# Reordered fill, drain and end of a two-layer graph-attention and expert kernel, with a merged routing softmax and moved attention products at the round borders

## What is computed

```python
x = x + gnn0(_layernorm(x), adj)   # masked attention over leaky_relu(f_i + f_j), softmax, @ Wh, elu
x = x + ffn0(_layernorm(x))        # per-token router (softmax, top 2 of 6), 6 experts of 3 layers, weighted
x = x + gnn1(_layernorm(x), adj)   # as gnn0 with other weights
x = x + ffn1(_layernorm(x))        # per-graph router on the mean token (top 2 of 8), gelu experts 128-256-128,
                                   # then a layer norm with gamma, beta
```

## Time and profile before

| | |
|---|---|
| median of 3 runs (lowest, highest) | 628.02 us (622.9, 629.22) |
| the profiled execution, its own time | 626.22 us |
| its span, first to last instruction | 624.2 us |
| PE busy / DVE / ACT / POOL | 563.5 (90%) / 459.6 (74%) / 411.5 (66%) / 233.8 (37%) us |
| steady body (mean of 12 between 95 and 405.2 us) | 25.85 us, PE busy 25.16, DVE 22.09, ACT 19.58 |
| tail, 16 groups | 7.14 us each, PE busy throughout |

### The profile page before, as it was taken

How to read it: one execution, slowest core, us unless ns; L and a number is a source line. 1 busy time by engine, 2 the same in 40 slices (tenths; PEclk the granted TensorE clock), 3 DMA queues, 4 the chain that set the end, 5 groups by cost and what they waited for, 6 DMA issues and landing times.

```text
span 624.2 us, 15150 instructions
## 1 busy us (share of the span) xinstructions
PE 563.5 (90%) x3830; PEld 455.1 (73%) x3831; DVE 459.6 (74%) x1714; ACT 411.5 (66%) x1099; POOL 233.8 (37%) x450
## 2 busy tenths in 40 slices
PE   5778999999999999999999999988966799999992
PEld 4555777777777777777777777766644599999992
DVE  2586778888898898988888888776453347777675
ACT  1244667767878678777777777857722178888782
POOL 5222213342434423344233442231332015666665
PEclk9988999999999999999999999999997799999997
DMA  8414225052250531404314043022000377777732
GB/s 189 95 37 153 66 89 154 2 153 72 83 152 1 151 98 54 152 15 137 101 51 152 10 142 102 1 104 102 1 1 1 93 244 217 231 220 223 216 112 67
DMA packets 78935, 66.19 MB, mean 106 GB/s; under 512 B 10018, under 2 KB 64562, under 8 KB 78898
## 3 DMA queue, kind: packets, MB, share of 16 engines
q1 hardware_dynamic: 65312, 59.78, 31.9%
q10 hardware_dynamic: 13586, 5.98, 3.6%
HBM read 61.31 MB, written 4.42 MB: 105 GB/s over the span
## 4 chain that ended last, share of the span: by engine, by line
PE 29%; DVE 17%; DMA 14%; issue 14%; ACT 13%; POOL 5%; SPq 5%; ACTq 1%; DVEq 1%; POOLq 0%
DMA x<-in_x 11%; PE bank L1547 4%; PE bank L1537 4%; SPq L612 4%; PE wide L1537 4%; PE wide L1547 4%; ACT p_xn L120 3%; PE bank L1340 3%; DMA w_scratch<-wrow 2%; PE bank L1353 2%; ACT h L785 2%; DVE h2w L1005 2%; DVE at_prT L317 2%; DVE route_stats L88 2%; ACT at_lk L284 2%
## 5 line engine op out<-in xcount | busy, mean ns | idle before, releaser
L1340 PE MATMUL bank<-h,w 128*128 128x512 f32 x192 | 101.4, 610 | 4.8 <-ACT h L790 4.8
L1353 PE MATMUL bank<-w,h2w 128*128 128x128 f32 x768 | 103.1, 278 | 0.0
L1353 PEld LDWEIGHTS bank<-w,h2w 128*128 128x128 f32 x768 | 95.0, 192 | 3.1 <-issue 1.0
L785 ACT ACTIVATE h<-bank,b 128x512 f32<-128x512 f32 x96 | 66.3, 690 | 43.8 <-PE bank L1340 43.8
L790 ACT ACTIVATE h<-bank,b 128x512 f32<-128x512 f32 x96 | 65.9, 687 | 27.6 <-PE bank L1334 27.6
L1005 DVE TENSOR_TENSOR h2w<-h,wide_w 128x512 f32<-128x512 f32 x96 | 65.1, 678 | 12.8 <-ACT h L785 12.6
L1332 PE MATMUL bank<-xnTh,w1h 128*128 128x512 f32 x96 | 67.3, 701 | 0.0
L101 POOL TENSOR_TENSOR route_var_eps<-route_mean_var,eps 128x4 f32<-128x4 f32 x16 | 10.9, 681 | 123.5 <-DVE route_mean_var L94 123.5
L101 POOL TENSOR_TENSOR at_var_eps<-at_mean_var,eps 128x4 f32<-128x4 f32 x32 | 12.3, 384 | 98.2 <-DVE at_mean_var L94 98.2
L269 ACT ACTIVATE at_pr<-at_lk,at_nm 128x128 f32<-128x128 f32 x128 | 41.1, 404 | 6.9 <-DVE at_nm L304 6.9
L240 PEld LDWEIGHTS wide<-at_wh,at_prT 128*128 128x128 f32 x256 | 31.9, 196 | 14.4 <-issue 5.2
(11 more groups left out here) (233 smaller groups left out, 1407.6 us busy)
## 6 DMA issues: line engine op xcount, KB each, us to landing
wide_w<-w_scratch SPq DMA_DIRECT2D x96, 256.0 KB, 4.5
mask<-in_L_ffn_W SPq DMA_DIRECT2D x128, 128.0 KB, 2.4
x<-in_x SPq DMA_DIRECT2D x16, 256.0 KB, 6.1
xin<-in_x SPq DMA_DIRECT2D x16, 256.0 KB, 6.2
adj_in<-in_adj SPq DMA_DIRECT2D x16, 256.0 KB, 6.3
wide_w<-bmix_scratch SPq DMA_DIRECT2D x14, 256.0 KB, 3.6
out<-at_pr ACTq DMA_DIRECT2D x8, 256.0 KB, 2.9
out<-at_prT ACTq DMA_DIRECT2D x8, 256.0 KB, 2.8
```

The costliest lines, as they stand in the source:

```text
L785: a.activation(h2[:, e % 2, :], b_h2[:, :], ACT.Relu, bias=b2[:, e:e + 1]).then_inc(h2_ready, 1)
L1340: pe.matmul(b_h2[:, :], w2[:, e, :], h1[:, e % 2, :], start=True, stop=True).then_inc(l2_done, 1)
L1353: last = pe.matmul(b_out[:, s], h2w[:, e % 2, s], w3[:, e, :], start=False, stop=(e == E0 - 1), skip_group_check=True)
```

## The change

It moves work and removes some; the mathematics stays. On the fill: the first group's transposes read x itself, so group 0 has no xin load; the four small weight tensors of the attentions are awaited alone (`EARLY` 4), the expert and router weights apart (`raw_loaded`); `split_w1`, `split_b3`, the statistics of groups 1 and 2 and the router's transposes of body 0 change places; POOL makes group 2's split ahead of the router's root; the copies of b3 are 3 DMAs and not 12. On the router: the copy `lg`, the pass `prob` and two of the three `wgt` passes go (`ROUTE` 14 to 13). At the border: at1's probabilities are transposed behind `layer2` of expert 0, and aggregated behind `layer3` of expert 5 and `layer1` of expert 1. On the drain: the max of group 15 goes ahead of group 14's pooled norm, group 15's ELU and residual are done in halves, and its `msum` comes from products of x with rstd plus the shift, and not from the normalized transposes. On the head: the choice is taken from the unnormalized exponentials; all of W1 is loaded into SBUF during the drain, and the first two graphs' matrices are copied from there by ACT; the gelu table is loaded ahead; bmix goes over SP. On the end: the last group is summed in halves, scaled by gamma while POOL makes rstd, and finished ahead of group 14.

```diff
+                if par >= 0:
+                    settle(sp, const_ready)
+                    need(sp, xin_loaded, 16 * (g - 1))
+                    need(sp, at0["xT_done"], g - 1)
+                    sp.dma_start(tiles(xin[:, par, :]), xg[g] if isinstance(g, int) else
+                                 xg[bass.ds(g, 1)].rearrange("a p t d -> p (a t) d")).then_inc(xin_loaded, 16)
...
-            load(0, 0)
+            load(0, -1)
...
+                sp.dma_start(b3[32 * q:32 * q + KW, :],
+                             A["L0_ffn_expert_b3"].unsqueeze(1).broadcast_to([E0, GG, P])).then_inc(small_loaded, 16)
...
+            sp.wait_ge(h2w_ready, N * E0)
+            sp.dma_start(w1r, A["L1_ffn_W1"].rearrange("e d f -> d e f")).then_inc(w1_resident, 16)
...
+            load_w1(0, 0, 2, 2)
+            sp.wait_ge(bmix_step, E1 + 3)
+            sp.dma_start(bmix_dram[:, :], bmix[:, :]).then_inc(bmix_stored, 16)
+            load_w1(1, 1, 0, 2)
+            sp.wait_ge(bmix_stored, 16)
+            load_bmix(0, 0)
+            load_w1(1, 1, 2, 2)
+            load_bmix(1, 1)
...
+                if i0 == 0:
+                    norm_root(rn, p, eps, minus_half, 1, rn["xn_ready"])
...
+            norm_root(fn, p, eps, minus_half, N - 1, fn["xn_ready"])
             finish(N - 2, 0)
-            norm_root(fn, p, eps, minus_half, N - 1, fn["xn_ready"])
-            finish(N - 1, 1)
...
+                a.dma_start(h2[:, 0, 0:RH], A["L0_ffn_router_w1"]).then_inc(raw_loaded, 16)
+                a.dma_start(h1[:, :, :].rearrange("p a f -> p (a f)")[:, 0:E0 * P],
+                            A["L0_ffn_expert_w1"].rearrange("e d h -> d e h")).then_inc(raw_loaded, 16)
...
+                if run:
+                    relu2(n, 0)
                 if live("attn1", i0, -1):
                     attn_act_prT(at1, a, i - 2)
-                if run:
...
+                if last(i0):
+                    for q in range(2):
+                        h = slice(2 * q * P, 2 * (q + 1) * P)
+                        a.wait_ge(at1["y_ready"], N + q)
+                        a.activation(at1["lk"][:, h], at1["y"][:, h], ACT.Exp).then_inc(at1["yexp_ready"], 1)
+                        a.wait_ge(at1["yexp_ready"], N + q)
+                        a.activation(at1["lk"][:, h], at1["lk"][:, h], ACT.Relu, bias=1.0, scale=-1.0)\
+                            .then_inc(at1["yneg_ready"], 1)
...
+                if i0 == -LEAD["route"]:
+                    a.wait_ge(wrow_done, 1)
+                    a.activation(wrow[:, :], b_misc[0:KB, 0:P], ACT.Copy).then_inc(wrow_ready, 1)
...
+            a.wait_ge(msum_done, 1)
+            a.activation(msum[:, NG - GG:NG], b_pool[:, 0:GG], ACT.Copy).then_inc(msum_ready, 1)
+            a.wait_ge(head_dve, 2)
+            a.activation(hd[:, 3, :], hd[:, 0, :], ACT.Exp, bias=hd[:, 2, 0:1]).then_inc(head_act, 1)
+            a.wait_ge(p_xnT_done, N)
+            a.activation(xnT3[:, cols(N - 1)], b_at0[:, :], ACT.Copy).then_inc(xnT3_ready, 1)
+            a.wait_ge(head_dve, 9)
+            a.activation(hd[:, 8, :], hd[:, 6, :], ACT.Exp, bias=hd[:, 2, 0:1]).then_inc(head_act, 1)
+            a.wait_ge(head_dve, 15)
             a.activation(hd[:, 11, 0:2], hd[:, 10, 0:2], ACT.Exp).then_inc(head_act, 1)
+            a.activation(hd[:, 10, 2:4], eps[0:NG, 0:2], ACT.Gelu)
...
+                if g0 == 0:
+                    a.wait_ge(w1_resident, 16)
+                    for t in range(2):
+                        for k in range(2):
+                            a.activation(w1c[:, t, k, :], w1r[:, bass.ds(picked[2 * t + k], 1), :]
+                                         .rearrange("p a f -> p (a f)"), ACT.Copy).then_inc(w1_loaded[t], 16)
...
+            for q in range(2):
+                a.wait_ge(fin_ready, N - 1 + q)
...
-                v.tensor_copy(lg[:, :, :], b_misc[:, 0:GG * E0].rearrange("p (t e) -> p t e", t=GG))\
-                    .then_inc(lg_ready, 1)
-                v.wait_ge(lg_ready, g + 1)
-                v.tensor_reduce(lgmx[:, :], lg[:, :, :], AX, ALU.max).then_inc(route_step, 1)
+                lg = b_misc[:, 0:GG * E0].rearrange("p (t e) -> p t e", t=GG)
+                v.tensor_reduce(lgmx[:, :], lg, AX, ALU.max).then_inc(route_step, 1)
...
-                v.tensor_tensor(prob[:, :, :], pe0[:, :, :], prc[:, :].unsqueeze(2).broadcast_to([P, GG, E0]),
-                                ALU.mult).then_inc(route_step, 1)
+                v.scalar_tensor_tensor(pd[:, :, :], pe0[:, :, :], -1.0,
+                                       prc[:, :].unsqueeze(2).broadcast_to([P, GG, E0]), ALU.add, ALU.mult)\
+                    .then_inc(route_step, 1)
...
-                for q in range(3):
-                    last = v.tensor_tensor(wgt[:, q, 0:KW].rearrange("p (e t) -> p t e", t=GG), pqs[:, :, :],
-                                           qrc[:, :].unsqueeze(2).broadcast_to([P, GG, E0]), ALU.mult)
-                last.then_inc(route_step, 1)
+                v.tensor_tensor(wgt[:, :, 0:KW].rearrange("p q (e t) -> p q t e", t=GG),
+                                pqs[:, :, :].unsqueeze(1).broadcast_to([P, 3, GG, E0]),
+                                qrc[:, :].unsqueeze(1).unsqueeze(3).broadcast_to([P, 3, GG, E0]), ALU.mult)\
+                    .then_inc(route_step, 1)
...
+                if i0 == -LEAD["attn0"]:
+                    split_w1()
+                if i0 == 0:
+                    measure(rn, 1, at0["x_ready"], 2)
+                    weight_low(0)
...
-                if i0 == -LEAD["route"]:
-                    split_b3()
...
-                if live("attn1", i0, -1):
-                    attn_dve_y(at1, v, i - 2)
...
+                if last(i0):
+                    v.wait_ge(at1["agg_done"], N)
+                    v.reciprocal(at1["rsum"][:, :], at1["parts"][:, :, 0]).then_inc(at1["rsum_ready"], 1)
+                    v.wait_ge(at1["rsum_ready"], N)
...
+                elif live("attn1", i0, -1):
+                    attn_dve_y(at1, v, i - 2)
...
+                if i0 == -LEAD["attn0"]:
+                    split_b3()
...
+                    if i0 == N:
+                        attn_dve_max(at1, v, N - 1)
...
+                if i0 == -LEAD["route"]:
+                    route_weights(0)
...
                 if i0 == -LEAD["route"]:
-                    weight_rows(i + 1)
+                    measure(at0["norm"], 2, x_loaded, 16 * 3)
+                    make_mask(2, 0)
...
-            softmax_end(h(8), h(9), 2, 2)
-            step(v.max(top8[:, :], h(9)))
-            step(v.max_index(top8i[:, :], top8[:, :], h(9)))
-            step(v.tensor_copy(pairs[:, 2:4], top8i[:, 0:2]))
-            step(v.tensor_scalar(h(10, 2), top8[:, 0:2], top8[:, 0:1], None, ALU.subtract))
-            spread_pairs(2)
+            v.wait_ge(head_act, 2)
+            step(v.max(top8[:, :], h(8)))
+            step(v.max_index(top8i[:, :], top8[:, :], h(8)))
+            v.tensor_copy(pairs[:, 2:4], top8i[:, 0:2]).then_inc(head_diag, 1)
+            step(v.tensor_reduce(h(2, 1), h(8), AX, ALU.add))
+            step(v.reciprocal(h(2, 1), h(2, 1)))
+            step(v.tensor_scalar(h(9, 2), top8[:, 0:2], h(2, 1), None, ALU.mult))
...
+            for t in range(GG):
+                s = slice(t * P, (t + 1) * P)
+                centred = v.scalar_tensor_tensor(sm[1][:, s], sm[1][:, s], fn["mv"][:, t, 0:1], gamma[:, :],
...
+            for q in range(2):
+                for t in range(2 * q, 2 * q + 2):
+                    s = slice(t * P, (t + 1) * P)
+                    half = v.scalar_tensor_tensor(fin[1][:, s], sm[1][:, s], fn["rstd"][:, t:t + 1], xb[1][:, s],
+                                                  ALU.mult, ALU.add)
+                half.then_inc(fin_ready, 1)
...
-            pe.wait_ge(wc_ready, 2)
...
+                if last(i0):
+                    busy_drain(i0, 18)
+                if live("attn1", i0, -1):
+                    attn_pe_transpose_probs(at1, pe, ident, i - 2)
+                if last(i0):
+                    pool_transpose(N, N)
+                    busy_drain(i0, 4)
+                if live("experts", i0, -1):
+                    layer3(n - 1, E0 - 1)
+                if run:
+                    layer1(n + 1, i, par, 1)
...
-                if run:
-                    layer1(n + 1, i, par, 1)
...
+                if i0 == 0:
+                    route_transpose(0, 0)
...
+                if pool and i0 < N:
                     pool_transpose(i, i0)
-                    busy_drain(i0, 4)
+                if last(i0):
+                    busy_drain(i0, 44)
+                    need(pe, xnT3_ready, N - 1)
+                    pe.matmul(b_pool[:, 0:GG], ident[:, :], zero[:, :, 0], start=True, stop=False, skip_group_check=True)
+                    pe.wait_ge(pn["rstd_ready"], N)
+                    for t in range(GG):
+                        pe.matmul(b_pool[:, t:t + 1], x[:, (N - 1) * GW + t * P:(N - 1) * GW + (t + 1) * P],
```

(16 more changed lines are left out.)

252 lines of the change are left out of this document (144 added, 108 removed).

## The result

The changed kernel takes 607.14 us (median of 4 runs, 604.68 to 609.18); the kernel before, 627.09 (4 runs). The ratio is 0.969, 95% interval 0.962 to 0.975. I had predicted 605 in a range of 597 to 613, with a sum of 21.9 us; the medians differ by 19.95, the two profiled executions by 17.0 (626.22 and 609.18). So sign and size were right. The terms behind the sum were not all right, and the experiments found that one of its main sentences, on what limits a round, was half the truth.

A forecast was written before the change was run, and what follows sets the result against it. It took the rounds to be bound by a loop through DVE's wrow and SP's x loads, not by PE, and the tail by PE. Terms summing to 21.9 off 626.2 gave 604.3, said as 605 us, range 597 to 613.

The forecast's parts named there:

- Term 1 to 3: Fill: earlier at_xT copy gains 2.2, moved split_b3 costs 0.7, POOL's order and smaller waits gain 3.3; 4.8 us together.
- Term 3: Fill: POOL's split of group 2 ahead of the router's root brings the first layer3 sooner; 3.3 us with smaller waits.
- Term 4: Rounds: DVE's shorter router passes save 0.2 us a body, 3 in all; the border move pays nothing there.
- rival B: Rounds: the loop does not get shorter, x's landing is fixed by the weight loads' queue; 608 us, chance 18%.
- rival D: Rounds: bodies fall to PE's own length, all 8.4 us of the loop gained; 599.5 us, chance 13%.
- Term 5: Last bodies, where PE rules: one product ahead of the transposes hides part of three at_pr waits; 2.5 us.
- Term 6: Drain: earlier max, halved ELU and residual, more fillers for the clock, mean tokens by short products; 7.3 us.
- Term 7: Head, router product to gidx: shorter chain gains about 1.8, 24 spacer products cost 2.7 at full clock; gain 0.7 us.
- rival C: Drain and head: PE stays at half clock, spacers cost 5.3 us, 3 to 4 lost; 608 to 609, chance 15%.
- Term 8: Head, gidx to first down: `up` starts no sooner, but down's wait for ACT and the table load go; 1.5 us.
- Term 9: End: halved sum and add, gamma beside POOL's rstd, last store no longer behind group 14's; 2.1 us.
- Rival E: Rounds: y of at1 waits for PE's later aggregation every round; 634 us if 2.7 a round, chance 4%.

The follow-up runs named there:

- its repeat: The changed kernel, unedited, timed once more later beside other runs on the same chip: 608.89 us, ratio 0.970 to the kernel before.
- x early: The changed kernel with each x load issued one body earlier: 594.49 us, ratio 0.949 with the new border; 610.19 us, 0.973 with the old.

## Why the prediction was right, and where it was not

*The sum* of 21.9 stands against 17.0 between the profiled executions and 19.95 between the medians. Fill, rounds and last bodies brought 1.5 more than I said, drain to end 6.5 less. That the median came within 2.1 us of 605 is in part luck: the two profiled executions are 3 us closer together than the medians, and terms 7 and 8 came with the wrong sign.

*Term 1 to 3, the fill* (4.8, came 5.7): the step "ACT cannot copy at_xT before its table load of 9.56 + 1.28 is over" failed. The load is itself behind ACT's DMA issues, one of which took 2.78 us before and 1.64 after, so the wall moved: 3.7 and not 2.2. The last of these issues in the kernel before and, in the second fence, in the changed one:

```profile
6.75 2.78 ACTq L776 DMA_DIRECT2D w<-in_L_ffn_expert_w  x1
```

```profile
6.52 1.64 ACTq L790 DMA_DIRECT2D w<-in_L_ffn_expert_w  x1
```

split_b3 cost 0.7 as said: from the start of the aggregation to the reciprocal of at_rsum 1.88 us against 1.20. Another 0.4 of the lead went ahead of it, where POOL's third pass of the split took 0.65 and not 0.23. Term 3 (3.3) came at about 3.0, and POOL's order alone carries 2.4 of it. Rival F did not come.

*Term 4, the rounds* (3, came 3.4): right in what it prices, 0.23 a body against 0.2, and so rival B fell. The 3.4 itself is no proof of it. From body 0 to body 13 the changed kernel takes 330.2 us and its repeat 330.5, but the run without spacers, whose rounds are the same, 326.1, with shorter x loads. The surcharge for reading PSUM that the prediction weighed is not seen: the subtraction of 24 elements takes 0.18 us from PSUM, and took 0.18 from SBUF before. The failing step is "In the loop rounds that pays nothing: the 0.58 a body are slack under the loop". A third of the bodies before stood already at PE's 25.6, with little or nothing of the x load above it, and with DVE's part shortened and the border left alone most came to rest there (seven of twelve). The move was needed for the gain to show: without it the time is 4.7 us longer, of which I had booked 2.5. Nor was PE's floor "25.16 and little more" (rival D): the busy time is no floor. With the old chain, waits and lost overlap come on top of it (25.6). With the new chain, x early, a body is 24.5 and the busy time itself has fallen to 24.4 (219.79 us in nine bodies). D itself did not come: x loads still set the bodies of the changed kernel.

*Term 5, the last bodies*: 2.5, came 2.7, and 2.4 by the run with the old border.

*Term 6, the drain* (7.3, came 6.1). Max ahead of the pooled norm: from group 15's scores to its transposes 7.91 became 5.28, 2.6 (2.4 said). The size was right by luck, for I took it from the twin's 2.09 and a gap, while what stood ahead of the max was this:

```profile
465.34 1.11 DVE L129 TENSOR_SCALAR p_xn<-x,pool_mean_var,pool_rstd 128x128 f32<-128x128 f32 x4 [1.48 <-POOL pool_rstd L104]
```

A pass of 1.11 and, ahead of it, a wait of 1.48 for POOL. Another 0.5 came ahead of the scores. Mean tokens by products: from pool_rstd to the router's product 5.70 became 2.70, 3.0 (2.8 said). The halves brought 0.4 and not 0.9: from at_y to pool_rstd 5.37 became 4.94. The fuller clock brought nothing in this execution: PE waited 1.89 ahead of the transposes, and from transposes to at_y 4.20 became 4.66, a loss of 0.5 where I had written a gain of 1.0. In the six executions in which the clock did not fall this stretch is 3.0, a gain of 1.2; as there is one trace of the kernel before, in which it fell, whether the change makes the fall rarer stays open.

*Term 7, the head* (0.7, came -1.9): the shortened chain was right, 6.14 to 4.96 without the spacers, 1.2 (1.8 said). The spacers' price was the choice "2.7 us at full clock", where the same sentence had 5.3 at half clock beside it. They ran at half clock and stuck out by 3.1. This is the part of rival C that came true, and it lies below my lower bound.

*Term 8* (1.5, came -0.5, less than the spread of 119.9 to 121.5 us from gidx to the last down among like executions): I wrote that `up` starts no sooner since ACT's copies take as long as the DMA did. All four copies were done 1.6 us ahead; the gate products stand ahead of `up` on PE, and their DVE inputs now come behind gidx, which makes that chain 4.0 us (2.9 before). What is late next was the question to ask there, and the order of PE's instructions behind gidx would have shown it. The early load of the gelu table (1.28) worked, and the first down no longer waits for ACT, but the time from gidx to it does not show it (10.07 before, 10.27 after).

*Term 9, the end* (2.1, came 1.4): the halves and the gamma pass worked, but DVE's last pass ran beside POOL's, 0.94 lost. A sign of this stood in the earlier trace rows: p_xn took 2.09, beside a POOL pass that began 0.6 us after it, and I took this for its price.

*Rival E* (DVE's y waits for the later aggregation) did not come: DVE's waits at at_rsum are 8.2 us in 12, and were 8.9 in 13, 0.68 each both times, all of them those of at0. The sign "over half a microsecond each round" was badly chosen, since the kernel before already had that.
